# Start of a fused transformer decoder layer: the split of a query weight ahead of the first input, a key weight's low part on GpSimd, two vector steps moved later

## The reference

```python
x = x + _L0_attn_ref(_layernorm(x), Wq, Wk, Wv, Wo)                  # rotary by token index, causal softmax
x = x + _L0_xattn_ref(_layernorm(x), ctx, pos, pos, Wq, Wkv, Wout, bout)  # q @ Wq, ctx @ Wkv, axial rotary
x = x + _L0_ffn_ref(_layernorm(x), gate, up, down)                   # silu(gate) * up, integer weights with scales
# axial rotary of the second attention:
freqs = ROPE_BASE ** (-jnp.arange(half, dtype=x.dtype) / half)
ang = pos[..., :, None] * freqs
cos = jnp.cos(ang)[:, :, None, :, :]
sin = jnp.sin(ang)[:, :, None, :, :]
```

## Time and profile before

| | us |
|---|---|
| runs of the kernel before, median | 1665.31 |
| lowest and highest of 3 runs | 1663.28, 1667.28 |
| the profiled execution, whole | 1663.07 |
| its span in the trace | 1661.3 |
| TensorE busy in the span | 1612.2 (97%) |
| VectorE, ScalarE, GpSimd busy | 1161.7 (70%), 967.0 (58%), 548.5 (33%) |

### The profile page before, as it was taken

How to read it: one execution, slowest core, us unless ns; L and a number is a source line. 1 busy time by engine, 2 the same in 40 slices (tenths; PEclk the granted TensorE clock), 3 DMA queues, 4 the chain that set the end, 5 groups by cost and what they waited for, 6 DMA issues and landing times. The chain is left out here.

```text
span 1661.3 us, 42062 instructions
## 1 busy us (share of the span) xinstructions
PE 1612.2 (97%) x15216; PEld 1265.6 (76%) x15216; DVE 1161.7 (70%) x2087; ACT 967.0 (58%) x3847; POOL 548.5 (33%) x535
## 2 busy tenths in 40 slices
PE   6899999999999999999999999998999999999997
PEld 4677777777777777777777777766888888888885
DVE  7788888888888888888888888777644344444332
ACT  6477777777777776777777777775422222222221
POOL 4344444444444444444444444431011011011011
PEclk9999999999999999999999999999999999999999
DMA  6111111101110101101111011024321020120110
GB/s 217 30 33 32 37 33 52 30 30 37 46 39 30 37 30 54 30 30 37 35 50 30 30 37 40 17 71 141 101 77 44 33 76 30 45 76 25 50 51 26
DMA packets 55098, 81.00 MB, mean 49 GB/s; under 512 B 4880, under 2 KB 25488, under 8 KB 55056
## 3 DMA queue, kind: packets, MB, share of 16 engines
q1 hardware_dynamic: 55056, 80.43, 14.9%
HBM read 63.63 MB, written 16.78 MB: 48 GB/s over the span
## 5 line engine op out<-in xcount | busy, mean ns | idle before, releaser
L949 ACT ACTIVATE prob<-bank,nmax 128x128 f32<-128x128 f32 x1536 | 539.9, 407 | 153.2 <-DVE nmax L1195 150.3
L949 ACT ACTIVATION_READ_ACCUMULATOR prob<-bank,nmax 128x1 f32 x1536 | 379.5, 247 | 0.0
L1606 PE MATMUL fbank<-shared,piece_hi 128*128 128x512 f32 x1152 | 280.3, 394 | 0.0
L1195 DVE TENSOR_REDUCE nmax<-bank 128x4 f32<-128x512 f32 x376 | 233.7, 684 | 47.4 <-PE bank L536 39.6
L1606 PEld LDWEIGHTS fbank<-shared,piece_hi 128*128 128x128 f32 x1152 | 215.8, 187 | 53.2
L399 POOL TENSOR_TENSOR rope_buf<-rope_buf 128x512 f32<-128x512 f32 x128 | 165.6, 1304 | 130.6 <-DVE rope_buf L1148 130.5
L1758 DVE SCALAR_TENSOR_TENSOR h<-fbank,su_c,sil 128x512 f32<-128x512 f32 x88 | 66.0, 750 | 200.6 <-PE fbank L1606 197.1
L1692 ACT ACTIVATE sil<-fbank,sg_c 128x512 f32<-128x512 f32 x88 | 60.5, 687 | 175.2 <-PE fbank L1606 172.2
L1698 ACT ACTIVATE h_h<-h 128x512 fp32r<-128x512 f32 x88 | 55.6, 632 | 175.3 <-DVE h L1758 175.3
L449 POOL TENSOR_TENSOR cn_l<-cn,cn_h 128x512 fp32r<-128x512 f32 x64 | 82.7, 1292 | 217.9 <-DVE cn L1187 217.9
L512 PE MATMUL bank<-shared,z1T_h 128*128 128x512 f32 x520 | 140.4, 412 | 4.2 <-ACT shared L932 2.6
(11 more groups left out here) (178 smaller groups left out, 3164.5 us busy)
## 6 DMA issues: line engine op xcount, KB each, us to landing
xA<-in_x SPq DMA_DIRECT2D x32, 256.0 KB, 3.1
xB<-in_x SPq DMA_DIRECT2D x32, 256.0 KB, 2.9
x_scratch<-x SPq DMA_DIRECT2D x32, 256.0 KB, 2.0
shared_loaded<-x_scratch SPq DMA_DIRECT2D x8, 1024.0 KB, 7.7
xr<-x_scratch SPq DMA_DIRECT2D x8, 1024.0 KB, 5.6
out<-xr SPq DMA_DIRECT2D x8, 1024.0 KB, 4.3
cx<-in_ctx SPq DMA_DIRECT2D x32, 128.0 KB, 2.2
range_window<-in_wg SPq DMA_DIRECT2D x27, 112.0 KB, 2.0
```

What stands on the lines that cost most here:

```text
L949: last = nc.scalar.activation(prob[:, c, i, :], S[c][:, i * P:(i + 1) * P], ACT.Exp, bias=nmax[:, c, i:i + 1], accum_out=rs[:, h:h + 1])
L1195: nc.vector.tensor_reduce(out=nmax[:, c, :], in_=S[c][:, :].rearrange("p (g k) -> p g k", g=G), op=ALU.max, axis=AX, negate=True).then_inc ...
L1606: last = nc.tensor.matmul(dst[:, :], w[:, k, cols], z[:, k, :], start=(n == 0), stop=(n == len(passes) * KT - 1))
```

## The change

Four edits, all before the third turn:

1. ScalarE splits q1 ahead of `z1T_high(0)`, and k1 and v1 ahead of the two sine instructions.
2. The low part of k1 is made by GpSimd instead of VectorE, in its preamble behind `rough_rstd(1, 0)`. It waits for two high parts, and raises a new semaphore `k1_lo`, for which TensorE waits in the k1 projection. The count of `w_lo` leaves k1 out.
3. VectorE makes the low part of q1 and `z1T_low(0)` first and `rotary_angles()` behind them. `rotary_table()` moves into turn A, behind the norm of sequence 1 and ahead of the low part of kv2.
4. The low part of q2 moves from before `add_self(0)` to behind the statistics of `x1A`.

```diff
+        k1_lo = sem("w_k1_lo_ready")
+        VECTOR_SPLITS = [n for n in ORDER if n != "k1"]
@@ gpsimd
             rough_rstd(1, 0)
+            pool.wait_ge(w_hi, 2)
+            pool.tensor_tensor(WLO["k1"][:, :, :], whole("k1"), WHI["k1"][:, :, :], ALU.subtract).then_inc(k1_lo, 1)
             pool.wait_ge(c_in, 32)
@@ tensor, project
-                        pe.wait_ge(w_lo, ORDER.index(name) + 1)
+                        if name == "k1":
+                            pe.wait_ge(k1_lo, 1)
+                        else:
+                            pe.wait_ge(w_lo, VECTOR_SPLITS.index(name) + 1)
@@ scalar
+            split_high(EARLY[:1])
             z1T_high(0)
-            split_high(EARLY[:1])
+            split_high(EARLY[1:])
             act.wait_ge(tab, 1)
             nc.scalar.activation(ang_s[:, :], ang_s[:, :], ACT.Sin).then_inc(tab_act, 1)
             nc.scalar.activation(ang_c[:, :], ang_c[:, :], ACT.Sin).then_inc(tab_act, 1)
-            split_high(EARLY[1:])
@@ vector, turn
                 if is_first(nx):
+                    rotary_table()
                     split_low(["kv2"])
...
                     rope("k1", nx, PA, DK1, cos1, sin1, 1.0)
-                    split_low(["q2"])
...
                     statistics(2, x1A, sq, between=k2_cos)
+                if is_first(sq):
+                    split_low(["q2"])
@@ vector, preamble
             normalise(1, xA, z1, 0)
-            rotary_angles()
             split_low(EARLY[:1])
             z1T_low(0)
-            split_low(EARLY[1:2])
-            rotary_table()
+            rotary_angles()
```

## The result

The changed kernel is slower. Over 20 runs its median is 1669.92 us (1666.84 to 1675.26), that of the kernel before in 20 runs 1665.01 (1660.63 to 1667.54); the ratio is 1.0033, 95% interval 1.0024 to 1.0041, so about 5.5 us (4.9 between the two medians) where +2.4 was forecast. The median lies in the stated range, the loss is more than twice the forecast, and not the likeliest case, "within 0.2%", came, but "slower by more", which had 0.31.

What follows compares the result with a forecast made beforehand. TensorE was taken as the bound from 100 us on, so its starts in the first 60 us decide. +1.65 + 0.75 + 0.87 - 0.2 - 2.14 + 1.8 - 0.3 = +2.4 us on 1665.31: 1667.7 us, 8-in-10 range 1664.2 to 1670.2.

Steps and rivals of the forecast that it cites:

- within 0.2%: Whole kernel: a time that differs from the kernel before by no more than 3.3 us; chance 0.62.
- slower by more: Whole kernel: slower by more than 0.2%, which is 3.3 us; chance 0.31.
- the lock: Start: GpSimd's k1 step, 12.1 to 16.8, shuts out VectorE's angle steps; q1's products at 19.9, +1.65 us.
- The collision: Turn A: sequence 1's norm on VectorE meets GpSimd's two context instructions; +0.75 us, between 0 and +1.3.
- the tables: Turn A: four table instructions come onto VectorE's chain to the row maxima, ahead of kv2's low part; +0.87 us.
- -0.3: Turn B, behind the keys: looser following work and part of the half clock at 50 to 52 us off the path; -0.3 us.
- rival 3: Turn B: half clock after a new pause before the keys' transposes slows second scores and q2; +4.2, 1669.5 us; chance 0.22.
- what a start gains or loses arrives whole at the end: From 100 to 400 us: TensorE, busy 299.13 of 300 us, never waits, so early shifts reach the end in full.

Runs made afterwards that it cites:

- the second experiment: The changed kernel with k1's low part back on VectorE, behind z1T_low and ahead of the angles: ratio 1.0021 to the kernel before.
- both ends filled: Kernel before and changed kernel, each with unread products in TensorE's pauses of turns A to C and at the attention phase's end: 1660.18 and 1663.59 us.
- the other filled pair: Kernel before and changed kernel, each with unread products in TensorE's pauses of turns A to C only: 1663.63 and 1663.59 us, ratios 0.9998 and 1.0002.

## Why the prediction was right and wrong

**Edit 1.** Right: 10.29 for 10.3, and the early start brought q1's products on VectorE no sooner, since VectorE took the result at 19.59.

**Edit 2, the lock.** Right in mechanism and size: GpSimd's step 12.12 to 16.70 (12.1 to 16.8), VectorE shut out from its first fast one-input step on, free at 19.6 instead of 19.9, so +1.36 for +1.65. TensorE's wait for k1's low part, put at nothing, was 0.42 us, and it was hidden. Its reason does not add up, though: from 10.3, sixteen products at 2.05 us for four end at 18.5, not 16.5; TensorE was ready at 16.33, as the later of them ran faster. The open question, whether fast one-input steps are shut out, is settled by the 4.69 us step, which is 0.29 again in the second experiment, where GpSimd has no step beside it, and by the 0.71 us table instruction there. The Trainium skill, "SBUF — State Buffer", section "SBUF: two separate sides", says that a VectorE step in a 2-port mode is kept out for the whole of GpSimd's instruction where that started first; the trace agrees, 4.69 us. By the number alone 19.3, the end without that rule, is as near to the measured 19.6 as 19.9 is; the 4.69 us step decides.

**The collision and the tables.** The norm's two steps took 0.56 and 0.58 us, for 0.22 and 0.16: +0.76 for +0.75. The tables took 28.05 to 28.98, +0.93 for +0.87. First row maxima +3.05 for +3.1.

**Edit 4.** The sum starts right behind o1 and the root waits at the lock, as written: x1A to the rotary sum's end is 5.8 us (52.32 to 58.10), 5.95 forecast. Together the waits give +2.59 in the row maxima of sequence 1 where both kernels run at full clock to there (both ends filled), and +2.79 in the other filled pair; the terms without the -0.3 add up to +2.7. The single terms above hold within 0.3 us.

**Where it failed.** The step is the clock: the term "-0.3" of edit 4, and with it the chance of 0.22 for rival 3. I let the half clock of 50 to 52 us become cheaper, where the change has a longer pause before v1's low part (3.30 us), one of 2.23 in the first attention and one of 2.92 before the keys. Two profiles of the change show it half for 20.5 and 13.7 us before 100 us, the profile of the kernel before for 6.8. With both ends filled the change costs 3.4 us, unfilled 5.5, so in place of -0.3 the clock's term is about +2; by the pair with the start alone filled it is the whole 5.5. That the half clock costs part of the 5.5 us is shown by both filled pairs; how large a part is not settled, since the pairs differ by 3.4 us.

Rival 3 had the right mechanism. Its sign, a granted clock of 0.5 after the keys, came (59.2 to 62.6 in the first profile of the change, 55.1 to 58.5 in the second). But its price was for one stretch in one place, and in the first profile the costliest fell on the first attention and the projections behind it, 38.7 to 48.9. The places move from run to run, by 3.7 us of effect at x1A. That its time, 1669.5, is so near to the measured 1669.92 is luck.

**The second failure** is in how the time was read. I took the places of the half clock in one execution of before, with 0.995 of the clock, as typical; its runs average 0.9925 to 0.9930 in the three later sets. And "what a start gains or loses arrives whole at the end" skipped the turns up to the last x1A, where some 1 us of the filled pairs' distance was given back, and the passage at 1100 to 1150 us, where the clock falls again: from the last x1A to the end it is 558.7 us in the profile of before and 561.2 in that of after, over the same instructions. That the start filled alone gave 0.9998 probably comes from this passage: in its profile that way takes 559.9 us.

## What to carry over

Before a step goes to GpSimd, look whether VectorE has two-input or fast one-input SBUF steps under it: here a 4.6 us step put on GpSimd to save VectorE 2.2 us cost it 4.4, and the first row maxima came 1.5 us later than without the offload. A long VectorE step with two SBUF inputs does not belong between a value that GpSimd waits for and GpSimd's reply, here 0.28% between two places. And where TensorE's pauses are some microseconds long, cost them twice, as idle time and as half clock behind them, or try to fill them with unread products: at the start alone that brought the kernel before nothing measurable, at both ends 0.3%. One profile does not show where the half clock falls in the next run.

## What had not been expected of the hardware

The half clock held for up to 10 us at a time, from 38.7 to 48.9 in the first profile of the change, while TensorE was busy (7.31 of 8 us from 40 to 48). The second profile of the same program has no half clock there. Filling pauses of the kernel before at both ends raised the mean granted clock from 0.9925 to 0.9969 and took 0.3% off its time; the unread products are the only difference.
